# Cross attention on one core: the second half's rounding work placed ahead of the next query's copy and low part

## The reference

```
q = einsum('bcn,dc->bnd', x, Wq) + bq          # 1024 x 64
k = einsum('bcn,dc->bdn', ctx, Wk) + bk        # 64 x 1024
v = einsum('bcn,dc->bdn', ctx, Wv) + bv        # 512 x 1024
attn = softmax(q @ k, axis=2)                  # 1024 x 1024, over the keys
out = einsum('bcm,bnm->bcn', v, attn) + x      # 512 x 1024
```

## Time and profile before

| what | value |
|---|---|
| median of 3 runs | 653.17 us |
| the profiled execution | 652.92 us |
| its span, first to last instruction | 651.1 us |
| PE busy | 643.3 us (99%) |
| DVE, ACT, POOL busy | 462.5, 335.1, 115.2 us |
| mean granted TensorE clock | 1.000 |

### The profile page before, as it was taken

One profiled execution on the slowest core, in us unless ns is written; L12 is line 12 of the kernel. 1 busy time (PEld: TensorE's weight loads), 2 busy tenths in 40 slices (PEclk: granted clock), 3 DMA queues, 4 the chain that ended last, 5 costly groups with the idle time before them and its releaser, 6 DMA issues.

```text
span 651.1 us, 9148 instructions
## 1 busy us (share of the span) xinstructions
PE 643.3 (99%) x3251; PEld 523.2 (80%) x3251; DVE 462.5 (71%) x509; ACT 335.1 (51%) x432; POOL 115.2 (18%) x50
## 2 busy tenths in 40 slices
PE   8999999999999999999999999999999999999997
PEld 6778788887888878888788887788788887888886
DVE  5897858757687677796676966869668687596541
ACT  6886546644456445474454653645626547275120
POOL 0022200431005400063000630006300143002000
PEclk9999999999999999999999999999999999999999
DMA  8903435962358622677317763187532964325352
GB/s 306 355 1 77 132 101 149 315 160 73 98 143 310 170 90 78 158 277 177 97 64 189 262 162 97 64 221 254 138 104 84 237 234 114 127 86 124 81 160 82
DMA packets 94254, 100.10 MB, mean 154 GB/s; under 512 B 7328, under 2 KB 69024, under 8 KB 94240
## 3 DMA queue, kind: packets, MB, share of 16 engines
q1 hardware_dynamic: 94240, 99.91, 51.2%
HBM read 51.64 MB, written 16.78 MB: 105 GB/s over the span
## 4 chain that ended last, share of the span: by engine, by line
PE 81%; DVE 8%; ACT 5%; issue 3%; DMA 1%; SPq 1%; ACTq 0%; DVEq 0%
PE acc_ps L972 33%; PE acc_ps L931 22%; PE acc_ps L988 9%; PE s_ps L884 8%; PE s_ps L900 5%; DVE q_st L587 3%; DVE pt_lo L587 2%; PE s_ps L892 1%; ACT pt_hi L350 1%; PE acc_ps L939 1%; PE s_ps L893 1%; DMA stage<-in_x_dram 1%; DVE full L591 1%; ACT cross L350 1%; ACT q_st L350 1%
## 5 line engine op out<-in xcount | busy, mean ns | idle before, releaser
L972 PE MATMUL acc_ps<-pt_hi,vt_hi 128*128 128x512 f32 x421 | 164.7, 391 | 1.9 <-DVE pt_lo L587 1.9
L972 PE MATMUL acc_ps<-pt_lo,vt_hi 128*128 128x512 f32 x421 | 163.9, 389 | 0.0
L972 PE MATMUL acc_ps<-pt_hi,vt_lo 128*128 128x512 f32 x421 | 163.8, 389 | 0.0
L313 POOL TENSOR_TENSOR pt_lo<-pt_raw,pt_hi 128x1024 fp32r<-128x1024 f32 x14 | 41.0, 2953 | 356.7 <-ACT pt_hi L350 356.7
L972 PEld LDWEIGHTS acc_ps<-pt_hi,vt_hi 128*128 128x128 f32 x421 | 79.0, 188 | 21.4 <-DVE pt_lo L587 4.3
L313 POOL TENSOR_TENSOR xs_lo<-stage,xs_hi 128x1024 fp32r<-128x1024 f32 x29 | 71.9, 2483 | 116.3 <-ACT xs_hi L350 115.8
L972 PEld LDWEIGHTS acc_ps<-pt_hi,vt_lo 128*128 128x128 f32 x421 | 79.0, 188 | 16.5
L972 PEld LDWEIGHTS acc_ps<-pt_lo,vt_hi 128*128 128x128 f32 x421 | 79.0, 188 | 16.1
L430 ACT ACTIVATE probs<-s_ps,negmax 128x1024 f32<-128x1024 f32 x56 | 62.5, 1115 | 51.1 <-DVE negmax L653 50.6
L653 DVE TENSOR_REDUCE negmax<-s_ps 128x1 f32<-128x1024 f32 x64 | 77.4, 1211 | 13.0 <-PE s_ps L902 11.2
L684 DVE STREAM_TRANSPOSE blocks<-probs 128x1024 f32<-128x1024 f32 x56 | 69.5, 1240 | 19.0 <-DMA pt_raw<-blocks 17.2
(11 more groups left out here) (133 smaller groups left out, 1145.6 us busy)
## 6 DMA issues: line engine op xcount, KB each, us to landing
pt_raw<-blocks SPq DMA_DIRECT2D x240, 128.0 KB, 2.4
stage<-in_x_dram SPq DMA_DIRECT2D x32, 512.0 KB, 6.2
o_sb<-in_x_dram SPq DMA_DIRECT2D x64, 256.0 KB, 3.4
out_dram<-o_sb SPq DMA_DIRECT2D x64, 256.0 KB, 2.5
stage<-in_ctx_dram SPq DMA_DIRECT2D x31, 512.0 KB, 8.6
pt_raw<-in_L_xattn_Wv_dram SPq DMA_DIRECT2D x4, 256.0 KB, 6.6
stage<-in_ctx_dram SPq DMA_DIRECT2D x2, 256.0 KB, 3.8
pt_raw<-in_L_xattn_Wk_dram SPq DMA_DIRECT2D x1, 128.0 KB, 2.9
```

The costliest lines, as they stand in the source:

```text
L313: return nc.gpsimd.tensor_tensor(out, src, hi.bitcast(F32), ALU.subtract)
L972: mm = nc.tensor.matmul(acc_ps[:, c % BANKS, :], v[:, m, cols], p[:, m, :], start=(m == 0 and v is vt_hi and p is pt_hi), stop=(m == MT - ...
```

## The change

On ACT, `q_second(nb)` (the two copies into `q_dup`) moves from ahead of the four roundings `p_hi(b, 1, j)` to behind them. On DVE, `q_low(nb)` moves from ahead of `low_x2(nb, 1)`, the four `p_lo(b, 1, j)` and `low_x2(nb, 3)` to behind them. Nothing is added or removed. The first seven batches have it, the last has none of these instructions.

```diff
@@ ACT, batch()
                     round_x2(nb, 2)
                     round_x2(nb, 1)
                     round_x2(nb, 3)
-                    q_second(nb)
                 for j in range(PAIRS):
                     p_hi(b, 1, j)
                 if last:
                     return
+
+                q_second(nb)
 
                 k_cross(nb)
                 k_high(nb)
@@ DVE, batch()
                 if not last:
                     dve.wait_ge(s_klo, nb * 2)
                     q_sum(nb)
-                    q_low(nb)
                     low_x2(nb, 1)
                 for j in range(PAIRS):
                     p_lo(b, 1, j)
                 if not last:
                     low_x2(nb, 3)
+                    q_low(nb)
                 out(b, 0, 2)
                 out(b, 0, 3)
```

## The result

| | before | with the change |
|---|---|---|
| median | 653.16 us (6 runs) | 649.02 us (6 runs, 648.93 to 650.92) |
| span of the profiled execution | 651.1 us | 647.4 us |
| PE busy, share | 643.3 us, 99% | 641.4 us, 99% |

The two medians are 4.1 us apart. The ratio is 0.9941, with a 95% interval of 0.9928 to 0.9954, which makes it 3.9 us less. The forecast was 649.1 us.

A forecast was written before the change was run, and what follows sets the result against it. TensorE was taken as the bound, busy 643.3 of 651.1 us, so only its waits could give time. Seven stalls summed to 3.95 us: 652.92 less 3.95 is 648.97, forecast as 649.1, range 648.5 to 651.0.

The forecast's parts named there:

- The bound and the place: TensorE's weight load waits 7 times for DVE's `pt_lo`, 4.3 us in all, at the start of half 1.
- The size of a stall: Loss over fifteen matmuls at half 1's start: 0.61 us batch 0, 0.59 batch 6, 0.55 in five others.
- That the stall goes: Half 1's first `pt_hi` starts at TensorE's release, 1.9 us earlier; `pt_lo` is ready with 1.2 us margin.
- The moved work: `q_low` and the `q_dup` copies, placed later, cost nothing until 4.9 us late.
- the cover: Time between `q_dup`'s end on ACT and the key's `cross` behind it: 3.5 us.
- slack in the key's chain: Time from `k_ll`'s end to the scores' start, behind the cover: 1.4 us more.
- The rule on the shared port: Two-input DVE and SBUF-reading POOL instructions exclude each other; moved `q_low` takes 0.68 us, `low_x2` of slice 1 inherits the block.
- Batch 0: Tighter: first `pt_lo` of half 1 has 0.6 us margin; if it fails, at most 0.61 us comes back.
- Rivals: Stall stays, 652.9 us, chance 0.05; part of the gain, 651, chance 0.05; and rivals 3 and 4.
- rivals 3 and 4: 3: TensorE stalls for pairs 1-3, 660.5 us, chance 0.05; 4: late key's chain, about 1 us a batch, 0.01.

## Why the prediction was right

- **The bound and the place.** TensorE's waits for `pt_lo` at the start of half 1 were the only thing the change could take, and they are gone. The reading of the earlier trace rows was right in sum and wrong in one detail. The seven waits of the weight load are six of 0.7 us at the starts of half 1 and one of 0.3 in batch 0's opening, which is still there after. Batch 0's wait of 0.7 was listed under "issue". The matmul side's seven are the seven places.
- **The size of a stall.** 0.55 to 0.61 us each, from the distance over fifteen matmuls. What stands behind the hole in that loss is mostly one distance: the second matmul of half 1 starts 0.34 us after the first, 0.11 more than 0.2267, and the following ones add a few hundredths. Batch 2's period fell by 79.47 - 78.92 = 0.55. From batch 0's stall to the end, the chain's last piece came 3.71 us earlier (604.31 to 600.60), and the head of this execution was 0.22 us later (58.82 to 59.04), so 3.93 were won where 3.95 were summed.
- **That the stall goes.** Forecast: the first `pt_hi` at TensorE's release, 1.9 us earlier, and a margin of 1.2 us. Measured: a release-bound start, and 1.3 us. One extra copy without effect, and a second that begins to cost, show it.
- **Which part does it.** The prediction took both moves together and did not say that ACT's alone would do. It is so, with 0.25 us to spare.
- **The moved work.** `q_low` at 0.69 and 0.68, `q_dup` ending at 237.08 and `cross` bound by TensorE with 3.4 us to spare, against 3.5 forecast. `out` of block 2 starts 19.35 us after the query projection (236.23 - 216.88), where it was 19.16 (236.98 - 217.82), so it did not quite start where it did. Nothing shows that this cost time. Behind the cover the prediction put 1.4 us of slack in the key's chain. Eight and ten copies bracket it: `q_dup`'s delay was hidden at one, and cost 1.1 us a batch at the other.
- **The rule on the shared port** (the Trainium skill, "SBUF — State Buffer", section "Who interferes with whom"). The trace after agrees with it, against the reading that 4.8 us is the own length of the two `q_low`: they lost nearly three quarters of their length (4.78 to 1.29 us for the pair) once they no longer ran beside POOL, and `xs_lo` took over the hold, 2.58 us for 1.23. The kernel with POOL cut short shows that without the hold the old order has no stall. That the hold comes from a shared port is the page's explanation; the runs show that it comes and goes with POOL's subtraction.
- **Batch 0.** Its first `pt_hi` waited for the data and started at 70.36; 70.05 was forecast, in the clock of before, and the head is 0.22 later. Its first `pt_lo` ends at 72.68 and the weight load starts at 73.16: a margin of 0.5 us, against 0.6 forecast. Its stall is gone too.
- **Rivals.** None occurred. The stalls of rivals 3 and 4 were brought about with added copies, and they set in where the margins of the prediction put them, but for batch 0 at m = 2. The prices hold for holes up to the 1.6 us seen without a fall of the clock. In the kernels with holes of 2.17 us and more the clock added to them.

No kernel here is clearly faster than the changed one. ACT's half alone and the old order with a shortened POOL reach the same time within their intervals. What is left of TensorE's waits for other engines lies in the first 50 us.

## What to carry to other kernels

An instruction that waits for a value nobody needs soon should not stand ahead of one that the bounding engine needs next. Count its wait too, and not only its length: here 0.61 us of idle time and two copies of 0.85 us stood ahead of the rounding. When work is moved off such a place, compute the margin of everything in its new order, since a gain ends where the margin begins. Another microsecond of head start was worth nothing here, and ACT's half of the change alone was enough. If a DVE instruction is several times as long as its twin elsewhere, look at what POOL does at that time.

## What the runs showed of the hardware that was not expected

TensorE's granted clock fell from 2.4 to 1.2 GHz at some of the long holes, though the engine was busy before and after. The holes are measured from one matmul's start to the next, in the profiled execution of each kernel. The seven holes of the kernel before (0.65 us, 0.73 in batch 0), of the one with three more copies (1.45, 1.61 in batch 0) and of the one with ten copies into `q_dup` (1.50) had no fall. Of seven holes of 2.17 us (2.34 in batch 0) three had one, of seven of 2.54 us (2.70 in batch 0) two, and of seven of 3.2 us two. A fall lasted some 3.4 us and cost 1.6 us where full-array matmuls followed. It began 0.6 to 1.0 us behind the holes of 2.17 us, at the end of those of 2.54, and still inside the hole of 3.2 us in batch 0, where the clock stayed down for 6.8 us:

```profile
91.00:91.80 0.80, 0.00 (x0) 0.00 (x0) 0.77 (x2) 0.07 (x1) 0.00 (x0) 1.00 0.00 0
91.85:98.65 6.80, 6.01 (x28) 5.18 (x30) 2.78 (x4) 2.35 (x3) 0.00 (x0) 0.50 0.26 77
98.70:100.00 1.30, 1.30 (x14) 1.12 (x12) 0.84 (x1) 0.00 (x0) 0.00 (x0) 1.00 0.00 0
```

The hole ends at 92.64. Why some batches have a fall and others, with the same hole, do not, stays open. It is not fixed by the kernel alone, as the four runs with twelve copies show.

The other finding is the pace behind a hole, with the clock at full speed. The first matmul takes 0.50 us for 0.39, the second starts 0.34 us after it, and the next six or so start 0.23 to 0.24 us apart and not 0.2267. Together this is 0.1 to 0.2 us a stall.
